# A graph-attention and mixture-of-experts kernel: the order of the router's work between the dense layers and the expert pieces

## What is computed

```
x = x + gnn(layernorm(x), h_target, adj)      # ends with: ht + gelu(ht @ W1) @ W2
n = layernorm(x)
logits = n @ gate_w.T                          # 8 numbers a row
top 2 of 8, softmax over the two
for e in range(8):
    y = gelu(n @ w1[e].T + b1[e]) @ w2[e].T + b2[e]
    out += comb[:, e] * y
x = x + out
```

## Time and profile before

| | us |
|---|---|
| median of three runs | 1043.12 |
| lowest and highest run | 1040.36, 1043.85 |
| the profiled execution | 1042.73 |
| its span in the profile | 1041.0 |
| PE busy | 942.9 (91%) |
| ACT busy | 727.0 (70%) |
| DVE busy | 673.5 (65%) |
| POOL busy | 548.3 (53%) |

### The profile page before, as it was taken

The page is one execution under the profiler, slowest core; times in us unless marked ns, Lnnn a source line. Parts: engine busy times, 40 slices in busy tenths (PEclk is TensorE's granted clock), DMA queues, the critical chain, the costliest instruction groups (busy, mean ns, idle before and its releaser), DMA issues.

```text
span 1041.0 us, 20744 instructions
## 1 busy us (share of the span) xinstructions
PE 942.9 (91%) x6686; PEld 571.4 (55%) x6750; DVE 673.5 (65%) x2002; ACT 727.0 (70%) x912; POOL 548.3 (53%) x485
## 2 busy tenths in 40 slices
PE   2778899999999999999999998889876899999993
PEld 1355444444444444444444454456655789989872
DVE  7659587888778887879787764455653734344331
ACT  4536799999999899998999983745324554555551
POOL 6647486666675767666576785100544422322311
PEclk9899899999999999999999998999986999999998
DMA  9596665753538544385557446571526232332323
GB/s 290 167 269 188 188 220 191 259 196 119 181 132 286 171 167 160 127 280 179 179 190 254 144 140 236 225 325 41 185 87 206 59 60 43 58 49 38 53 34 96
DMA packets 74298, 168.43 MB, mean 162 GB/s; under 512 B 13586, under 2 KB 42386, under 8 KB 68242
## 3 DMA queue, kind: packets, MB, share of 16 engines
q1 hardware_dynamic: 50354, 97.99, 29.0%
q0 software_dynamic: 19984, 67.93, 21.8%
q10 hardware_dynamic: 3856, 1.19, 0.5%
HBM read 120.84 MB, written 61.96 MB: 176 GB/s over the span
## 4 chain that ended last, share of the span: by engine, by line
PE 74%; DVE 10%; ACT 4%; DMA 4%; issue 3%; SPq 2%; POOL 1%; ACTq 0%; POOLq 0%; DVEq 0%
PE ps L1785 13%; PE ps L1808 12%; PE ps L1822 11%; PE ps L1948 10%; PE ps L1960 9%; PE ps L1810 9%; DVE masked L1069 2%; PE ps L1876 2%; PE ps L1864 2%; PE ps L1839 1%; DMA cT<-ctx_cols 1%; PE ps L1759 1%; DVE maskA L1031 1%; ACT wall L1615 1%; SPq L452 1%
## 5 line engine op out<-in xcount | busy, mean ns | idle before, releaser
L1069 DVE CUSTOM_DVE_ANT_0 masked<-ps,maskA 128x512 f32<-128x512 f32 x512 | 346.3, 688 | 108.5 <-PE ps L1785 106.1
L1585 ACT ACTIVATE masked<-masked,negmax 128x2048 f32<-128x2048 f32 x128 | 256.7, 2005 | 33.5 <-DVE negmax L1075 30.5
L1688 ACT ACTIVATE weights<-ps 128x1024 f32<-128x1024 f32 x256 | 248.8, 1010 | 33.0 <-PE ps L1810 32.5
L1785 PE MATMUL ps<-ks,qs 96*128 96x512 f32 x512 | 257.1, 536 | 14.9 <-DVE piecemax L1069 9.1
L1808 PE MATMUL ps<-qs,ks 98*128 98x512 f32 x512 | 227.2, 503 | 3.1 <-DMA qs<-shift_lo 2.8
L1810 PE MATMUL ps<-maskB,identb 128*128 128x512 bf16 x448 | 176.9, 395 | 0.0
L1785 PEld LDWEIGHTS ps<-ks,qs 96*128 96x128 f32 x512 | 99.0, 193 | 99.1 <-DVE piecemax L1069 77.2
L955 POOL DMA_INDIRECT sum_rows<-y,ids x39 | 60.2, 1544 | 154.8 <-DVE y L1300 131.0
L1822 PE MATMUL ps<-weights,v_all 128*32 128x256 f32 x2048 | 137.9, 387 | 0.9 <-ACT weights L1688 0.9
L795 POOL TENSOR_SCALAR maskB<-adjB 128x1024 bf16<-128x1024 int32 x32 | 116.6, 3643 | 37.9 <-DMA adjB<-in_adjT 34.6
L1282 DVE TENSOR_TENSOR gT<-ffn_w,gT 128x2048 f16<-128x2048 f32 (+1 forms) x23 | 45.2, 1967 | 120.2 <-ACT gT L1642 120.2
(11 more groups left out here) (230 smaller groups left out, 1123.1 us busy)
## 6 DMA issues: line engine op xcount, KB each, us to landing
expert_rows<-pad_rows POOLq DMA_DIRECT2D x73, 272.0 KB, 5.9
split_weights<-whl POOLq DMA_DIRECT2D x36, 512.0 KB, 3.5
adjA<-in_adj SPq DMA_DIRECT2D x16, 1024.0 KB, 7.3
adjB<-in_adjT SPq DMA_DIRECT2D x32, 512.0 KB, 5.8
wall<-split_weights SPq DMA_DIRECT2D x16, 1024.0 KB, 15.6
wch<-in_w1T POOLq DMA_DIRECT2D x14, 512.0 KB, 5.8
wch<-in_w2T POOLq DMA_DIRECT2D x14, 512.0 KB, 6.1
xr<-expert_rows SPq DMA_DIRECT2D x16, 272.0 KB, 2.8
```

What stands on the lines that cost most here:

```text
L1069: dve.tensor_tensor_reduce(masked[:, a % 2, k * 512:(k + 1) * 512], ps[:, u % 2, :], maskA[:, a, k * 512:(k + 1) * 512], 1.0, NO_EDGE, ALU ...
L1585: act.activation(masked[:, a % 2, :], masked[:, a % 2, :], ACT.Exp, bias=negmax[:, h % 2, a:a + 1], accum_out=rowsum[:, h % 4, a:a + 1]).t ...
L1688: act.activation(weights[:, j % 4, :, :], ps[:, 2 + 2 * (j % 2):4 + 2 * (j % 2), :], ACT.Exp).then_inc(weights_ready, 1)
L1785: pe.matmul(ps[:, u % 2, :], qs[0:KR, h % 4, a * P:(a + 1) * P], ks[0:KR, h, k * 512:(k + 1) * 512], start=True, stop=True)\
```

## The change

Six things are moved; nothing is added to or taken from the computation.

1. PE: `ranks(1)` goes from behind `hidden(3, 4)` to behind `hidden(3, 6)`. DVE: `send(1)` goes from behind `split_hidden(3, 4)` to behind `split_hidden(3, 5)`.
2. ACT: `normalise_x(2)` stood as four activations behind piece 6; now two stand behind piece 4 and two behind piece 5.
3. PE: `gates(2)` goes from behind `back(3, 0)` to ahead of it, `ranks(2)` from behind `back(3, 2)` to behind `back(3, 1)`, and `gates(3)` from ahead of `turn_rows(0)` and `turn_rows(1)` to behind them.
4. POOL: `scatter(2)` is written in one run of eight; before, `row_factors(1, 3)` stood between its fourth and fifth DMA.
5. DVE: `choose_first(3)` and `choose_second(3)` go behind `low_rows` and `keep_meta` of pieces 0 and 1.
6. DVE: `final_table()` goes from ahead of the loop over the pieces to the end of its first round, behind `weigh(0)` and `keep_meta(2)`.

```diff
--- before.py
+++ after.py
@@ -821,11 +821,11 @@
                     pool.wait_ge(gap_ready, b + 1)
                     pool.tensor_tensor(gap[:, 1, :], euler[:, :], gap[:, 0, :], ALU.pow).then_inc(gap_exp, 1)
 
-                def scatter(b, tiles=range(TPB)):
+                def scatter(b):
 
                     pool.wait_ge(rows_ready, 2 * b + 2)
                     pool.wait_ge(slots_ready, 2 * b + 2)
-                    for a in tiles:
+                    for a in range(TPB):
                         for k in range(TOPK):
                             pool.indirect_dma_start(
                                 out=expert_rows[:, :], in_=rows_of[b][:, a, :], in_offset=None,
@@ -932,9 +932,8 @@
                 gap_power(1)
                 scatter(1)
                 gap_power(2)
-                scatter(2, range(0, 2))
+                scatter(2)
                 row_factors(1, 3)
-                scatter(2, range(2, TPB))
                 gap_power(3)
                 for q in range(2):
                     for a in range(2):
@@ -1499,7 +1498,7 @@
                         choose_first(1)
                     elif f == 2:
                         choose_second(1)
-                    elif f == 4:
+                    elif f == 5:
                         send(1)
                 choose_first(2)
                 choose_second(2)
@@ -1512,15 +1511,14 @@
                 new_stats(3, (2, 3))
                 new_moments(3)
                 early_table()
-                choose_first(3)
-                choose_second(3)
                 dve.memset(credit4[:, 0:1], 0.0).then_inc(y_ready, 1)
                 for j in range(2):
                     low_rows(j)
                     keep_meta(j)
+                choose_first(3)
+                choose_second(3)
                 send(3)
                 low_hidden(0)
-                final_table()
                 dve.wait_ge(c_in, 32)
                 for j in range(SLOTS):
                     if j + 2 < SLOTS:
@@ -1530,6 +1528,8 @@
                     weigh(j)
                     if j + 2 < SLOTS:
                         keep_meta(j + 2)
+                    if j == 0:
+                        final_table()
 
             @block.scalar
             def _(act):
@@ -1595,10 +1595,10 @@
                 def normalise_h(b, tiles=range(TPB)):
                     normalise(0, b, hb[:, b, :, :], hb[:, b, :, :], h2_normed, tiles)
 
-                def normalise_x(b):
+                def normalise_x(b, tiles=range(TPB)):
                     if b == 3:
                         act.wait_ge(scattered[1], 16 * TOPK * TPB)
-                    normalise(1, b, xb[:, b % 2, :, :], rows_of[b], xn_ready)
+                    normalise(1, b, xb[:, b % 2, :, :], rows_of[b], xn_ready, tiles)
 
                 def high_turned(b):
                     for c in range(DC):
@@ -1716,8 +1716,8 @@
                 copy_xnT(1)
                 for f in range(FC):
                     hidden_high(3, f)
-                    if f == 6:
-                        normalise_x(2)
+                    if f in (4, 5):
+                        normalise_x(2, range(2 * f - 8, 2 * f - 6))
                 copy_xnT(2)
                 normalise_x(3)
                 copy_xnT(3)
@@ -2059,19 +2059,18 @@
                         gates(1)
                 for f in range(FC):
                     hidden(3, f)
-                    if f == 4:
+                    if f == 6:
                         ranks(1)
                 turn_xn(2)
+                gates(2)
                 for a in range(TPB):
                     back(3, a)
-                    if a == 0:
-                        gates(2)
-                    elif a == 2:
+                    if a == 1:
                         ranks(2)
                 turn_xn(3)
-                gates(3)
                 for j in range(2):
                     turn_rows(j)
+                gates(3)
                 pe.wait_ge(experts_in, 32 * E)
                 pe.wait_ge(table_ready, 2)
                 this = expert(pe, 0)
```

## The result

The change takes **1049.11 us** (median of 14 runs, 1045.77 to 1053.07) and the kernel before, on the same chips, 1042.57 us (14 runs, 1037.89 to 1046.10). The ratio is 1.0063, with a 95% interval of 1.0049 to 1.0078: slower by 6.5 us. The forecast was 1046.8 us, the range 1043.0 to 1050.0. So sign and range held; the forecast lies 2.3 us low and the time 0.9 under the range's upper end.

What follows compares the result with a forecast made beforehand. The prediction took PE, busy 91% of the span, as the bound; -0.9 + 1.1 + 0.8 - 2.93 + 4.3 + 1.7 = +4.07 us on the profiled 1042.73 gave 1046.8 us, range 1043.0 to 1050.0.

Steps and rivals of the forecast that it cites:

- The second place: The long table: -2.93 us before `first_half(2)`, +4.3 waiting before `turn_rows(4)`, +1.7 for the clock behind that wait.
- the signs that the prediction names for being wrong: `turn_rows(4)` without a wait, or `first_half(0)` before 794 or after 799.
- the rival with the faster number and rows: Piece 4's number and rows come faster than 3.6 us after the table: 1045.8 or 1046.7 us; chance 0.04.
- `gates(3)` on the path: Start of the experts: `gates(3)` now stands between the rows and the first piece, its own 3.58 us on the path.
- The earlier writes: POOL's `scatter(2)` ends at 783.6, 4.5 us earlier; with `gates(3)` on the path, the first piece starts only 0.9 earlier.
- The clock at `gates(2)`: PE's clock may fall in a gap of some 2.5 us before `gates(2)`: from nothing to +2.0 us, taken +1.1.
- The first piece's clock: More of `first_half(0)`'s first 24 matmuls may run at 1.2 GHz: at most 1.9 us, at best 0.9 gained, taken +0.8.
- the first place: The start of the experts, which POOL's writes set: -0.9 us for the start, +1.1 and +0.8 for the clock.
- both upper ends: Both places at their highest cost, together +7.8 us: 1050.5 us; chance 0.10.
- The clock holds at both new waits: Rival without the clock falls behind the two new waits: +1.3 us, 1044.0, no change that can be told; chance 0.27.
- full clock when the rows land: Rival: PE at full clock when piece 1's rows land; the first place gives -4.0 us, total 1040.1 us; chance 0.06.

Runs made afterwards that it cites:

- e1: The kernel before with only the long table's move to the end of the loop's first round: 1045.33 us against 1043.18, ratio 1.0026.
- e6: e2 with `scatter(2)` again in two halves, the factors of block 3 between them, `gates(3)` still behind the rows: 1044.96 us against 1042.51, ratio 1.0029.
- e7: e5 with `scatter(2)` again in two halves and the factors of block 3 between them: 1043.18 us against 1043.24, ratio 0.9996.
- e5: e2 with `gates(3)` ahead of `turn_rows(0)` and `turn_rows(1)` again, as before: 1042.82 us against 1043.24, ratio 0.9989.
- e2: The change with the long table back at its old place ahead of the loop: 1047.44 us against 1043.18, ratio 1.0047.
- e2_again: The same program as e2, measured once more: 1045.25 us against 1042.51, ratio 1.0024.
- e8: e2 with the store of x1's last block behind the loads of pieces 0 and 1 on SP: 1041.06 us against 1043.24, ratio 0.9977.
- e4: The change with 18 unread matmuls of 128x512 filling the wait before `turn_rows(4)`: 1046.75 us, ratio 1.0028 to the kernel before.
- e11: e8 with the long table in two parts, behind `low_rows(2)` and behind `keep_meta(2)`: 1040.43 us against 1042.51, ratio 0.9984.

## Why the prediction held, and what was mis-sized

The second place held by its mechanism, the first only in part. One of the signs that the prediction names for being wrong came: `first_half(0)` after 799. It started at 801.76, and without the 2.43 us that were there before the change began at 799.33; `scatter(2)` ended at 788.00, so counted 785.57, not near 784. That the time still lies in the range owes to the range's width.

- **The second place held.** No wait before `first_half(2)`; 4.04 us before `turn_rows(4)` (predicted 4.3, e1 4.11), by the steps given: piece 0's weighing behind piece 1's hidden layer, the table, 0.8 to the issue, the landing. From the table's end to PE's work on the rows it is 835.62 - 832.01 = 3.6 us, as in the sum, so the rival with the faster number and rows falls. The clock fell behind it: 2.4 us, the upper end, where I took 1.7. e1 alone measures 2.7 us (1.3 to 4.2) against the forecast 3.1.
- **`gates(3)` on the path held.** Predicted at its own 3.58 us; its time there is 3.42, and taking it away gave 3.4 us by ratio and 3.1 by the rows (e6 against e7). e5 is no second proof, as its gates are still on the path.
- **The earlier writes were mis-sized**, and this is the step that failed: "Piece 1's rows were transposed 795.83 - 788.15 = 7.68 after that end, so now from 791.3 to 792.4." The distance was taken as constant. It was 797.58 - 788.00 = 9.58 in the change, 1.9 more, of which 1.7 are the last write's landing in 4.1 instead of 2.4 us beside the store of x1. `first_half(0)` came 2.2 later than the sum has it: these 1.9, 0.9 by which the writes ended later than at 784.7 (783.6 and the clock's 1.1), less 0.5 from the rows to the first piece. The text counted SP's sets and stores among what costs nothing, since they go out earlier too; they do, by 0.4 us, and the writes by 2.6.
- **The clock at `gates(2)`** was a term of +1.1 between 0 and +2.0. In the change `gates(2)` took 3.58, and `send(2)` came at +28.58 where the sum has 770.1 or 770.5, some +26.7, and the clock's +1.1: 0.8 later. No profile shows the +1.1 that I took: `send(2)` comes at +27.1 in e2, e2_again, e6 and e8 and at +28.6 in the change, e4, e5, e7 and e11, some 0.4 or 1.9 over the sum's +26.7.
- **The first piece's clock** was taken at +0.8 and measured +1.3 in this profile (upper end +1.9).
- **Sum.** By ratios the first place cost 3.7 us, not 1.0, and the second 2.7, not 3.1; the 3.7 holds the fall in e2 that the change does not have. The rival "both upper ends" had the right direction; its 1050.5 lies 1.4 above the median. "The clock holds at both new waits" and "full clock when the rows land" fell: in the change the clock was low at all three places.

## What to carry to other kernels

A write that is moved earlier keeps its time to landing only if the queues beside it are as empty at the new time: look up what else is in flight there, and move that store behind the loads that the path needs. An operation that lies in a wait costs its whole time once it stands behind what is waited for, however small it is; put back ahead, it is hidden only if its own operand comes early enough (e7, not e5). And where two consumers wait for parts of one long step, its move only moves the wait; cut the step where an idle stretch ends.

## What was not expected of the hardware

The same wait did not have the same price each time. Behind 2.11 us of waiting `gates(2)` took 1.95 us, at full clock, in three profiles of the change's order (e2, e6, e8), 3.58 or 3.59 in five (change, e4, e5, e7, e11) and 2.29 in one (e2_again). But the clock fell in all nine: where the gates kept it, it fell in the 48 matmuls behind them, which took 7.07 us instead of 5.40. From the start of the gates to the second half of the layer it is 9.1 us in e2, e2_again, e6 and e8 and 10.5 in the five; before, where the gates stand behind the first 24 matmuls, gates, 48 matmuls and ranks take 7.3. In the four it was a profile with an early block 3 (first layer at 741.0 to 741.6), in the five a late one (743.5 to 746.3); that is seen, not explained.

The prediction's rule, that 2.93 us before `first_half(2)` leave the clock alone, came from one profile: before, e5 and e6 show it (48 matmuls in 5.41), e2, e2_again, e7 and e8 don't (7.08, 6.82, 6.82, 6.72). In the three the first 24 matmuls of `first_half(0)` had taken 3.69 to 4.31, in the four 4.93 to 5.28. Behind the 4 us before `turn_rows(4)` the clock fell both times (7.32, 6.72).

The Trainium skill (TensorE: Matmul & The Clock Gate, Part 1 on the HAM clock gate) states that the number of slow matmuls of one kernel differs from run to run. These profiles agree: what differs among them is how much ran slowly, and each of them alone would have given a rule.
